# Cross-attention and feed-forward on one core: float32 projections for the first row, paired probability products, a last row in halves

## What is computed

```python
def attn(q, k, v):                       # k = v = ctx_1024
    qh = split_heads(q @ Wq.T + bq) / math.sqrt(16)
    kh = split_heads(k @ Wk.T + bk)
    vh = split_heads(v @ Wv.T + bv)
    attn = softmax(einsum('bhqd,bhkd->bhqk', qh, kh), axis=-1)
    return einsum('bhqk,bhkd->bhqd', attn, vh) ... @ Wo.T + bo
x = x + attn(layernorm(x), ctx_1024, ctx_1024)
xg = layernorm(x).reshape(8, 512, 256)   # one group of weights for each row
h1 = einsum('gmh,goh->gmo', xg, W1) + b1
h2 = einsum('gmo,gho->gmh', h1, W2) + b2
x = x + h2
```

## Time and profile before

| | us |
|---|---|
| median of 3 runs | 600.4 (598.92 to 601.99) |
| the profiled execution | 602.24 |
| its span, first to last instruction | 600.4 |
| TensorE busy | 549.4 (91%) |
| VectorE busy | 444.3 (74%) |
| ScalarE busy | 378.6 (63%) |
| GpSimd busy | 282.1 (47%) |
| granted TensorE clock, mean | 0.955 |

### The profile page before, as it was taken

How to read it: one execution, slowest core, us unless ns; L and a number is a source line. 1 busy time by engine, 2 the same in 40 slices (tenths; PEclk the granted TensorE clock), 3 DMA queues, 4 the chain that set the end, 5 groups by cost and what they waited for, 6 DMA issues and landing times.

```text
span 600.4 us, 13277 instructions
## 1 busy us (share of the span) xinstructions
PE 549.4 (91%) x4211; PEld 328.6 (55%) x4211; DVE 444.3 (74%) x809; ACT 378.6 (63%) x692; POOL 282.1 (47%) x367
## 2 busy tenths in 40 slices
PE   7699999899899989899899989999889989889987
PEld 7455436556455546465455556555455546344576
DVE  6697896889668886889668886889668885884033
ACT  4225768677577658667576668776576765767700
POOL 5214722736466292736456192746556290316501
PEclk9857999999899999999899999999899998997979
DMA  8730333362254344362264343262264233330200
GB/s 293 209 80 2 90 89 109 82 221 69 84 134 161 91 126 108 73 228 54 74 156 155 92 124 106 57 229 53 87 160 160 55 90 95 89 140 3 88 2 36
DMA packets 34081, 65.31 MB, mean 109 GB/s; under 512 B 9778, under 2 KB 11642, under 8 KB 31994
## 3 DMA queue, kind: packets, MB, share of 16 engines
q1 hardware_dynamic: 34042, 64.81, 36.7%
HBM read 34.65 MB, written 4.44 MB: 65 GB/s over the span
## 4 chain that ended last, share of the span: by engine, by line
PE 43%; POOL 22%; issue 22%; DVE 7%; ACT 3%; DMA 1%; POOLq 1%; SPq 1%; DVEq 0%; ACTq 0%
PE pv L505 10%; PE st L491 8%; PE misc L568 7%; PE nat L474 5%; PE misc L581 5%; POOL b_part L1242 3%; POOL b_part L1239 2%; POOL y L1227 2%; POOL ctx_lo L1214 2%; PE misc L620 2%; POOL rstd L1169 2%; DVE neg_max L944 2%; POOL y L1220 2%; POOL b_part L1246 2%; POOL b_part L1234 2%
## 5 line engine op out<-in xcount | busy, mean ns | idle before, releaser
L944 DVE TENSOR_REDUCE neg_max<-nat 128x1 f32<-128x512 f32 x512 | 335.7, 681 | 100.7 <-PE nat L474 98.8
L788 ACT ACTIVATE probs<-st 128x512 f32<-128x512 f32 x505 | 290.7, 597 | 155.0 <-PE st L491 146.4
L474 PE MATMUL nat<-ks,qs 63*128 63x512 f32 x512 | 248.0, 515 | 5.9 <-DVE neg_max L944 4.3
L491 PE MATMUL st<-qs,ks 64*128 64x512 f32 x505 | 240.1, 498 | 14.4 <-ACT probs L788 13.7
L491 PEld LDWEIGHTS st<-qs,ks 64*128 64x128 f32 x505 | 93.5, 190 | 131.6 <-ACT probs L788 106.9
L505 PE MATMUL pv<-probs,vs 128*32 128x512 f32 x1024 | 139.8, 619 | 1.0 <-ACT probs L788 0.7
L474 PEld LDWEIGHTS nat<-ks,qs 63*128 63x128 f32 x512 | 96.8, 195 | 19.7 <-DVE neg_max L944 12.4
L620 PE MATMUL misc<-w_in 64*128 64x256 f32 x512 | 73.9, 391 | 0.0
L1220 POOL TENSOR_TENSOR y<-y,bo_all 128x256 f32<-128x256 f32 x32 | 22.5, 736 | 92.2 <-DMA y<-x 92.2
L620 PEld LDWEIGHTS misc<-w_in 64*128 64x128 f32 x512 | 49.7, 190 | 15.5 <-issue 9.7
L1166 POOL TENSOR_SCALAR var_eps<-mean_var 128x4 f32<-128x4 f32 x16 | 3.6, 226 | 93.5 <-DVE mean_var L961 93.0
(11 more groups left out here) (159 smaller groups left out, 711.7 us busy)
## 6 DMA issues: line engine op xcount, KB each, us to landing
w_in<-w SPq DMA_DIRECT2D x8, 1024.0 KB
w_in<-w2T SPq DMA_DIRECT2D x8, 1024.0 KB
ks<-hi SPq DMA_DIRECT2D x64, 128.0 KB, 2.4
qs<-hi SPq DMA_DIRECT2D x64, 128.0 KB, 2.4
x_in<-x SPq DMA_DIRECT2D x8, 512.0 KB, 3.5
ctx_in<-ctxT SPq DMA_DIRECT2D x8, 512.0 KB, 3.4
ks<-lo SPq DMA_DIRECT2D x32, 128.0 KB, 2.4
qs<-lo SPq DMA_DIRECT2D x32, 128.0 KB, 2.4
```

What stands on the lines that cost most here:

```text
L474: mm(ring(at)[:, :], qs[rows, 2 * g + jj, c * P:(c + 1) * P], ks[rows, 2 * g + jj, :], start=True, stop=True).then_inc(nat_done, 1)
L491: mm(st_of(u, prep)[:, :], ks[rows, 2 * g + jj, kc * P:(kc + 1) * P], qs[rows, 2 * g + jj, :], start=True, stop=True).then_inc(st_done, 1)
L788: act.activation(probs[kc % 2][:, j, :], st_of(u, prep)[:, :], ACT.Exp).then_inc(exp_done, 1)
L944: dve.tensor_reduce(neg_max[:, g % 2, col:col + 1], ring(at_nat(n))[:, :], AX.X, ALU.max, negate=True).then_inc(max_done, 1)
```

## The change

It has these parts:

- **First row.** K, Q and V of row 0 are plain float32 products of unsplit operands (`qk_first`, `v_first`); SCALE goes into the copy of the transposed x and no longer into Wq, in all rows. x comes in two halves, weights have a semaphore each, an exponential on one element stands first on ScalarE. hi and lo of the first half of K and Q are made from PSUM, the others by GpSimd from raw. DMAs are issued in a new order. 24 nat tiles are made before the turn, the last 18 with a pair of products on other banks between them (`keep_warm`), and half of V's products among the first.
- **Paired pv.** Two groups of probability products run one behind the other at every eighth unit, and probs has four buffers.
- **b2.** b2_part is multiplied in one step of 2048 columns and added up in three; it is summed over partitions in four 64-row products of 128 columns among the w21 pieces (18 now), and copied in two halves. b2_parts stands before add_b2 on GpSimd, add_bo last.
- **ctx and other queues.** The context of row b + 2 is loaded at the head of turn b and split at unit 42. SyncE's and GpSimd's orders and the units of all pieces are changed; the last turn has a SyncE and a GpSimd order of its own.
- **Last row.** The first half of the output projection and x + bo (by a product with the identity) go into the units 60 to 63. What follows goes in two halves of the tokens: combination, sums, spread inverse, product, projection, statistics (read from PSUM), root, norm, transposes, copies. Fewer warm-up products stand between; the output leaves in three DMAs.

The diff, cut to its core:

```diff
-FIRST_LEAD = 26
+FIRST_LEAD = 24
...
-K_AT = (3, 3, 4, 4, 4, 5, 8, 8, 8, 8, 9, 9)
-Q_AT = (11, 12, 12, 12, 13, 13, 15, 15, 16, 16, 17, 17)
-WO_AT = (18, 19, 20, 20, 23, 24, 25, 25)
-V_AT = (29, 29, 29, 29, 31, 32, 32, 33)
-YT_AT = (36, 37)
-Z_AT = (39, 39, 41, 41, 43, 43, 44, 44)
-W21_AT = (48, 51, 52, 53, 55, 55, 56, 57, 58, 58, 59, 60, 60, 60, 61, 61)
-B2_UNIT = 48
-
-EVEN_AT = (20, 52)
-MASK_AT = (25, 58)
-ODD_AT = (36, 2)
-PAIR_AT = (39, 6)
-INVERT_AT = (51, 7)
-Y_NORM_AT = (30, 33)
-CTX_AT = 57
-X_STATS_AT = (28, 41)
-X_AGGREGATE_AT = 47
-X_NORM_AT = (54, 59)
+K_AT = (2, 3, 3, 4, 4, 5, 6, 7, 7, 8, 8, 8)
+Q_AT = (11, 12, 12, 13, 13, 13, 15, 15, 15, 16, 16, 17)
+WO_AT = (19, 20, 21, 21, 22, 23, 24, 24)
+V_AT = (27, 28, 29, 29, 30, 31, 32, 32)
+YT_AT = (34, 34)
+Z_AT = (36, 36, 37, 38, 39, 39, 40, 41)
+W21_AT = (44, 44, 45, 46, 48, 49, 51, 52, 53, 54, 55, 55, 56, 58, 59, 60, 61, 62)
+
+EVEN_AT = (21, 50)
+MASK_AT = (27, 53)
+ODD_AT = (38, 2)
+PAIR_AT = (45, 12)
+INVERT_AT = (47, 7)
+Y_NORM_AT = (32, 32)
+CTX_AT = 42
+X_STATS_AT = (39, 49)
+X_AGGREGATE_AT = 53
+X_NORM_AT = (58, 58)
...
-        probs = [sb(f"probs{i}", [P, 4, S]) for i in range(2)]
+        probs = [sb(f"probs{i}", [P, 4, S]) for i in range(4)]
...
                 if post:
                     stack_quad(b, 3)
+                if load:
+                    wait_apart(sp, ctx_ready, b + 1)
+                    load_ctx(b + 2)
+                if post:
                     gather_sums(b - 1, 1)
                 store_max(b, 1)
                 if post:
                     save_inverse(b - 1, 1)
-                    spread_inverse(b - 1, 1)
                     wait_apart(sp, w21_done, 2 * b)
                     wait_apart(sp, b2_part_ready, b)
                     load_ffn(b)
+                    spread_inverse(b - 1, 1)
+                if prep:
+                    stack_quad(b + 1, 0)
                 store_max(b, 2)
+                if prep:
+                    stack_quad(b + 1, 1)
                 if load:
                     wait_apart(sp, norm_ready[0], 4 * (b + 2))
                     load_x(b + 2)
-                if prep:
-                    stack_quad(b + 1, 0)
                 gather_sums(b, 0)
-                if prep:
-                    stack_quad(b + 1, 1)
                 store_max(b, 3, prep)
-                if load:
-                    wait_apart(sp, ctx_ready, b + 2)
-                    load_ctx(b + 2)
+                save_inverse(b, 0)
                 if post:
                     store_out(b - 1, 0)
                     store_out(b - 1, 1)
-                save_inverse(b, 0)
                 if prep:
-                    store_max(b + 1, 0)
                     stack_quad(b + 1, 2)
                 load_y(b)
                 spread_inverse(b, 0)
-
-            def load_w(which, src, done):
-                sp.dma_start(w_in[:, which], src.rearrange("(f p) d -> p f d", p=P)).then_inc(done, 16)
-
-            load_x(0)
+                if prep:
+                    store_max(b + 1, 0)
...
+            def keep_warm(n):
+
+                for t in range(2):
+                    rows = slice(HALF * t, HALF * t + HALF)
+                    mm(misc[2 + t][:, :], hi[rows, 1, 0, 0:P], hi[rows, 0, 0, :], start=True, stop=True)
...
-                              probs[n % 2][:, j, :], start=(kc == 0), stop=(kc == 3),
+                              probs[n % 4][:, j, :], start=(kc == 0), stop=(kc == 3),
...
+            def qk_first(which, m, f):
+
+                last = mm(misc[4 * (1 - which) + m][:, :], w_in[:, (WQ, WK)[which], f, m * P:(m + 1) * P],
+                          (xT_raw, ctx_in)[which][:, f, :], start=(f == 0), stop=(f == F - 1))
...
-                phase, o = i // OC, i % OC
+                phase, o = i // (OC + 1), i % (OC + 1) - 1
                 for t in order(phase):
                     f, rows = t ^ phase, TILES[t]
-                    last = mm(misc[f][:, 0:D], w1_in[rows, o, f * P:(f + 1) * P], w2_in[rows, o, :],
-                              start=(i == 0 and not (b2 and f == 0)), stop=(i == 2 * OC - 1), skip_group_check=True)
+                    if o < 0 and b2:
+                        mm(misc[f][:, D:D + P], ones[rows, :], b2_part[rows, 0, f * P:(f + 1) * P],
+                           start=(phase == 0), stop=False, skip_group_check=True)
+                    if o >= 0:
+                        last = mm(misc[f][:, 0:D], w1_in[rows, o, f * P:(f + 1) * P], w2_in[rows, o, :],
+                                  start=(phase == 0 and o == 0 and not b2), stop=(i == 2 * OC + 1),
+                                  skip_group_check=True)
...
-                    if u % 4 == 2:
-                        if u > 4:
-                            pv(b, u // 4 - 1)
-                        elif post:
-                            pv(b - 1, 15)
+                    if u % 8 == 2:
+                        for n in (u // 4 - 2, u // 4 - 1):
+                            if u > 8:
+                                pv(b, n)
+                            elif post:
+                                pv(b - 1, 16 + n)
+                    if u == UNITS - 2 and not prep:
+                        pv(b, 14)
                     jobs(b, u, post, prep)
+                    if not prep and LAST_WO_AT <= u < LAST_WO_AT + 2:
+                        if u == LAST_WO_AT:
+                            pe.wait_ge(attn_ready, 2 * LAST + 1)
+                            pe.wait_ge(max_done, RING * B + 1)
+                        for c in (2 * (u - LAST_WO_AT), 2 * (u - LAST_WO_AT) + 1):
+                            last_half(c, True, attnT[:, 0, c * P:(c + 1) * P], wo_in[:, 0, :])
+                    if not prep and LAST_X_AT <= u < LAST_X_AT + 2:
+                        if u == LAST_X_AT:
+                            pe.wait_ge(xbo_ready, B)
+                        for c in (2 * (u - LAST_X_AT), 2 * (u - LAST_X_AT) + 1):
+                            last_half(c, False, ident[:, :], y[:, c, :])
...
+            pe.wait_ge(ctx_loaded, 16)
+            pe.wait_ge(w_loaded[WK], 16)
             for f in range(F):
-                qk(0, 0, FIRST_BANKS[0], f)
+                qk_first(1, 0, f)
             xT(0, 0, 2)
             xT(0, 1, 3)
+            qk_first(1, 1, 0)
+            pe.wait_ge(xT_ready, 2)
+            pe.wait_ge(w_loaded[WQ], 16)
             for f in range(F):
-                qk(0, 1, FIRST_BANKS[1], f)
-            pe.wait_ge(xT_ready, 2)
-            pe.wait_ge(w_ready, 2)
-            for i in (2, 3):
-                for f in range(F):
-                    qk(0, i, FIRST_BANKS[i], f)
-            pe.wait_ge(w_ready, 3)
-            for c in range(C):
-                v(0, c, 6 + c // 2)
-            pe.wait_ge(lo_ready, 4)
-            pe.wait_ge(dve_set, 5)
-            pe.wait_ge(v_ready, 2)
+                qk_first(0, 0, f)
+            qk_first(1, 1, 1)
+            for f in range(F):
+                qk_first(0, 1, f)
+            pe.wait_ge(w_loaded[WV], 16)
+            pe.wait_ge(first_lo, 1)
+            for i in range(4):
+                v_first(i)
+            pe.wait_ge(first_lo, 2)
+            pe.wait_ge(first_raw, 2)
...
+                if 2 <= n < 6:
+                    v_first(n + 2)
+                elif n > 5:
+                    keep_warm(n)
...
+            stay_warm(3, 4)
             for c in range(C):
+                if c % 2 == 0:
+                    pe.wait_ge(last_comb, c // 2 + 1)
                 last = mm(misc[LAST_SUMS_BANK][:, 8 * c:8 * c + 8], odd_sum[:, c * P:(c + 1) * P],
                           pick[:, :, :].rearrange("p j t -> p (j t)"), start=True, stop=True)
             last.then_inc(last_sums, 1)
+            stay_warm(2, 4)
+            for c in range(C):
+                half = c // 2
+                if c % 2 == 0:
+                    pe.wait_ge(last_recip[half], 1)
+                last = mm(misc[LAST_HALF_BANKS[half]][:, c * P:(c + 1) * P],
+                          even_sum[:, c * P:(c + 1) * P], ident[:, :], start=True, stop=True)
+                if c % 2:
+                    last.then_inc(last_inv, 1)
+            pe.wait_ge(odd_out, 2 * B)
+            for half in range(2):
+                pe.wait_ge(last_attn, half + 1)
+                for c in (2 * half, 2 * half + 1):
+                    last = last_half(c, False, attnT[:, 1, c * P:(c + 1) * P], wo_in[:, 1, :])
+                last.then_inc(last_wo, 1)
             pe.wait_ge(out_ready, 2 * LAST)
             pe.wait_ge(w21_ready, B)
             pe.wait_ge(b2_part_ready, B)
             for c in range(C):
+                at = c % 2 if c < 2 else 0
+                mm(misc[LAST_Z_BANKS[c]][:, at * D:(at + 1) * D], ones[:, :], b2_part[:, 0, :],
+                   start=(c != 1), stop=False, skip_group_check=True)
+            stay_warm(6, 7)
+            last_turn(0)
+            stay_warm(2, 7)
+            pe.wait_ge(last_yT, 2)
+            last_out(0)
+            last_turn(1)
```

(21 more changed lines are left out.)

475 lines of the change are left out of this document (262 added, 213 removed).

## The result

The changed kernel takes 585.45 us (median of 4 runs, 583.45 to 586.16) where the kernel before, on the same chip, takes 601.08: ratio 0.974, 95% interval 0.9702 to 0.9778. The forecast was 552, with a range of 538 to 568: the sign is right, and two thirds of the gain are missing. The profiled execution took 583.45 (span 581.7).

What follows compares the result with a forecast made beforehand. Turns were taken as bound by TensorE's program order, VectorE 14 us behind. Prologue 35.2, turn 0 60, six turns 378.4, turn 7 59 and tail 19.5 sum to 552.1 us; forecast 552, range 538 to 568.

Steps and rivals of the forecast that it cites:

- the sentence on SyncE's queue: Full turn, SyncE: what the new load order passes is harmless; spread_inverse stands 2 us later, still ahead of unit 19.
- such dips: Full turns: TensorE's granted clock falls to 0.52 after waits for the b2 sum; their end saves 0.7 us a turn.
- b2: Full turn, GpSimd: eleven steps become five, 9.2 us for 11.2, starting before add_b2; TensorE's 1.9 us wait goes.
- The +0.5 for add_b2: Full turn: out_half on VectorE waits 0.1 to 1 us for GpSimd's add_b2, now behind b2_parts; taken as +0.5 us.
- ctx: Full turn: earlier load, split at unit 42 and subtraction before add_bo make ctx_lo ready in time; 1.33 us go.
- Pairs: Full turn: pairing probability products takes away 8 of 16 breaks of 0.35 us, at most 2.8; 1.4 us taken.
- replaced one for one, at nothing: Full turn: the pieces' new places, bq and SCALE moved into the xT copy cost nothing; the pairs' bound covers unevenness.
- Rival A: Pairs give all of 2.8 us a turn, with no wait for add_b2: 61.2 per turn, 539 us; chance 0.20.
- rival B: Pairs starve the other engines, each costing 0.1 to 0.2 us where VectorE or ScalarE set the pace: 571 us; chance 0.17.
- Turn 7: Last turn: pairs give 0.5 to 1 us, a clock dip 1.5, float32 output and x products cost 1.2 to 2: 59.
- Turn 0: First turn, 62.00 us before: keep_warm gives 2.2, two more early row maxima 1.2, pairs 0.8: 60.2, rounded 60.
- Prologue and tail: Before turn 0 and after turn 7: 35.2 us, 6.5 earlier, and 19.5 us, 8.0 less, including 1 for a clock dip.

Runs made afterwards that it cites:

- fixed: The changed kernel with one edit, SyncE issuing spread_inverse(b-1, 1) ahead of load_ffn(b) as the kernel before did: 556.05 us, ratio 0.9261.

## Why the prediction missed

By its own steps; "fixed" is the kernel with the spread first:

| stage | forecast | changed | fixed |
|---|---|---|---|
| prologue | 35.2 | 35.8 | 35.5 |
| turn 0 | 60 | 58.2 | 58.2 |
| turns 1 to 6 | 378.4 | 401.1 | 377.1 |
| turn 7 | 59 | 69.7 | 66.3 |
| tail | 19.5 | 16.9 | 17.0 |
| span | 552.1 | 581.7 | 554.1 |

**The step that failed** is the sentence on SyncE's queue, "spread_inverse stands behind four parameter loads (2 us), still ahead of unit 19". It priced what is moved past by its issue time (2 us, which the trace bears out: 239.54 to 241.61), and the four loads carry 2 MB, so that the division comes 4.7 us later and not 2, and TensorE stands at unit 19. Shown by both kernels that move this step alone: 29 us one way, 34 the other. In the changed kernel's full turns the price is 4.0: 2.85 is the wait for attnT (17.1 in turns 1 to 6), and the other 1.1 goes with the clock behind it. Behind turn 4's wait:

```profile
317.50:321.50 4.00, 3.88 (x21) 3.76 (x22) 1.38 (x2) 1.51 (x3) 3.61 (x4) 0.57 0.19 45
```

It fell so behind the wait in turns 1, 2, 4 and 5, and these are longer than in the fixed kernel by their wait and 1.1 to 1.9 us. In turns 3 and 6, behind waits of 2.79 and 2.04, it stayed at 1.00, and these are longer by their wait and 0.2. I had taken 0.7 a turn out of the sum for such dips because the b2 wait went; the new wait brought them back.

**b2** was right: b2_parts takes 9.0 us (250.48 to 259.49 in turn 3 of the fixed kernel) where 9.2 was forecast, its multiply 3.60 where 3.8 was, and no wait is left; with add_b2 ahead of it the wait comes back. The +0.5 for add_b2 is 0.43 on TensorE. Not forecast: the second copy of b2_all on ScalarE makes the next transposes wait 0.5 a turn (L608 <- b_all); I had said ScalarE has room, which is true of the turn and not of its last units, where it has 7.4 us of work in 8.

**ctx** was right in what goes. Of its causes the unit on ScalarE is out; the order on GpSimd is what is left, untested.

**Pairs** were mis-sized as a term: 3.15 a turn rather than 1.4. What was wrong behind it is the line that new places of pieces are "replaced one for one, at nothing". On the old places pairs gain nothing in a full turn; the new places without pairs give 66.0, 1.5 more than the 64.5 that my other terms leave of 68.2. The two together take 64.5 to 62.85, that is 1.65: as a joint term my 1.4 was near, as a price of pairs it was not. That a full turn of the fixed kernel comes out at 62.85 for 63.1 is therefore in part luck, two errors that cancel. Rival A had the size of a pair in a stretch in which TensorE has no idle time, rival B (the exponentials starve behind a pair where ScalarE has other work) the behaviour on the old places; the prediction treated them as exclusive, and each holds in its own stretches.

**Turn 7** is the second miss, 7.3 us even in the fixed kernel. Its last six units take 12.65 us for 8.87 before. With single products in this turn, and so with as many groups in these units as before, they take 11.82: the output and x products cost 2.95, where I had 1.2 to 2, and the group that pairs move there 0.8. TensorE's timeline of the fixed kernel:

```profile
530.55 1.13 PE L584 MATMUL nat<-wo_in,attnT 128*128 128x256 f32 x4
531.61 0.50 PE L545 MATMUL nat<-qs,ks 64*128 64x512 f32 x1
532.04 1.07 PE L559 MATMUL pv<-probs,vs 128*32 128x512 f32 x8
...
533.67 1.13 PE L584 MATMUL nat<-y,ident 128*128 128x256 f32 x4
```

ScalarE there:

```profile
532.15 0.60 ACT L865 ACTIVATE probs<-nat 128x512 f32<-128x512 f32 x1 [1.32 <-PE nat L545]
```

Each of the four units has 1.06 us of these products, start to start, and ScalarE stands idle for 1.32: it hides nothing, since the score products queue behind them. The sum's -1.5 for a dip of the clock didn't come (0.95 over the turn, 0.94 before), and the pairs gave nothing. Part of it is work that left the tail. The units ahead of the last six take 53.8 us for 51.3 before, and 53.5 without pairs; the cause of these 2.5 us stays open.

**Turn 0** took 58.2 where I had 60; 0.9 of that is its group less, which I hadn't seen.

**Prologue and tail** were right within 0.6 and 2.6 us. First nat 19.90 (20.4), first row maximum 20.41 (21). In the tail the granted clock is 1.00, so the dip of 1 us didn't come either.

## What to carry to other kernels

A step moved past DMA issues is moved past their bytes: price it by what the loads ahead carry, against the room of whoever waits for it, and keep a small transfer that a chain hangs on ahead of bulk loads that nobody needs soon. A saving on the busiest engine has its own size only in the stretches in which that engine has no idle time; elsewhere it was nothing, a loss, or more than its size where it took a wait away. So cut a turn into stretches before multiplying. A wait has a second price if the clock falls behind it, and it comes with the new wait as it went with the old one.
